# PSUM double buffering in a two-stage attention and expert kernel: wait for the reader of the own bank, not for the newest reader

## The reference

```python
xn = layernorm(x)
# recurrent stage: 8 heads of 128
q, k, v = xn @ Wq.T, xn @ Wk.T, xn @ Wv.T
o = chunked_linear_attention(q, k, v)          # causal, running state
o = rmsnorm(o / max(|sum(q * cumsum(k))|, 1))
s = o @ Wo.T
# gate stage
h1 = rmsnorm(xn) * g1
q = h1 @ fWq; c = h1 @ fWdkv                   # 1024 and 512 wide
k = c @ fWuk; v = c @ fWuv                     # 16 heads of 64
h2 = xn + softmax(causal(q @ k.T / 8)) @ v @ fWo
h3 = rmsnorm(h2) * g2
comb = softmax over the 2 best of 8 of (h3 @ gate_w), else 0
h4 = h2 + sum_e comb[:, e] * (silu(h3 @ w1[e]) @ w2[e])    # hidden 2048
y = x + s * silu(h4)
```

## Time and profile before

| | us |
|---|---|
| median of two runs | 6832.09 |
| the two runs | 6691.96, 6972.22 |
| profiled execution | 6699.76 |
| its span, slowest core | 6698.2 |
| spans of the 8 cores | 6643.8 to 6698.2 |
| TensorE matmuls busy | 3353.7 (50% of the span) |
| TensorE weight loads busy | 1259.4 (19%) |
| ScalarE busy | 1153.4 (17%) |
| VectorE busy | 1110.9 (17%) |
| GpSimd busy | 43.7 (1%) |

### The profile page before, as it was taken

How to read it: one execution, slowest core, us unless ns; L and a number is a source line. 1 busy time by engine, 2 the same in 40 slices (tenths; PEclk the granted TensorE clock), 3 DMA queues, 4 the chain that set the end, 5 groups by cost and what they waited for, 6 DMA issues and landing times.

```text
span 6698.2 us, 41992 instructions; the slowest of 8 cores (6643.8 to 6698.2 us)
## 1 busy us (share of the span) xinstructions
PE 3353.7 (50%) x13297; PEld 1259.4 (19%) x13297; DVE 1110.9 (17%) x2130; ACT 1153.4 (17%) x1783; POOL 43.7 (1%) x65
## 2 busy tenths in 40 slices
PE   0443333465233333333333447777777777777770
PEld 0221111211000000000001212222222222222220
DVE  4003333002222222222222210000000000000002
ACT  3221010110222222222222111110111111111111
POOL 0000000000000000000000000000000000000000
PEclk9976666675555555555555779998999999999995
DMA  4110000200000000000001120202020202020104
GB/s 151 35 25 10 13 13 13 41 13 7 0 0 0 0 0 0 0 0 0 0 0 28 43 43 1 50 0 51 0 51 0 51 1 51 3 49 15 36 1 150
DMA packets 56024, 158.52 MB, mean 24 GB/s; under 512 B 4224, under 2 KB 5248, under 8 KB 55808
## 3 DMA queue, kind: packets, MB, share of 16 engines
q0 software_dynamic: 39248, 95.54, 7.8%
q1 hardware_dynamic: 16560, 60.30, 2.6%
HBM read 209.42 MB, written 33.55 MB: 36 GB/s over the span
## 4 chain that ended last, share of the span: by engine, by line
PE 50%; DVE 16%; ACT 15%; issue 10%; DMA 6%; DVEq 1%; ACTq 1%; SPq 0%; POOLq 0%; PEldq 0%
PE ps L145 48%; ACT p2pb L803 7%; ACT p3hid L1012 5%; DVE p2rlf L831 3%; DVE acc L1031 3%; DMA p4s<-s_sp 1%; PE pt L150 1%; DMA p0x<-x 1%; DVE p2pb L815 1%; DVE p2pb L813 1%; DVEq L73 1%; DVE p1o1f L528 1%; PE pw L145 1%; DVE p2tmp L759 1%; DVE p2omla L846 1%
## 5 line engine op out<-in xcount | busy, mean ns | idle before, releaser
L145 PE MATMUL ps<-h3T,p3w 128*128 128x512 bf16 x4096 | 982.8, 383 | 435.2 <-ACT p3hid L1012 432.8
L145 PE MATMUL ps<-p3w,p3hid 128*128 128x512 bf16 x4096 | 935.5, 382 | 278.3 <-DVE acc L1031 241.7
L1012 ACT ACTIVATE p3hid<-ps 128x512 bf16<-128x512 f32 x512 | 305.7, 597 | 2276.8 <-PE ps L145 2276.8
L145 PE MATMUL ps<-p2pb,p2vaug 128*65 128x512 bf16 x640 | 302.0, 627 | 749.5 <-DVEq L96 414.3
L1031 DVE SCALAR_TENSOR_TENSOR acc<-ps,p3comb,acc 128x512 f32<-128x512 f32 x256 | 192.1, 750 | 2431.8 <-PE ps L145 2427.9
L145 PEld LDWEIGHTS ps<-h3T,p3w 128*128 128x128 bf16 x4096 | 369.1, 98 | 1043.5 <-issue 694.4
L803 ACT ACTIVATE p2pb<-ps,p2nmub 128x512 bf16<-128x512 f32 x640 | 439.9, 687 | 663.5 <-PE ps L145 617.7
L145 PEld LDWEIGHTS ps<-p3w,p3hid 128*128 128x128 bf16 x4096 | 384.5, 98 | 829.2 <-issue 428.3
L145 PE MATMUL ps<-p2qT,p2kT 64*128 64x512 bf16 x640 | 300.1, 622 | 138.8 <-DVEq L96 138.1
L145 PEld LDWEIGHTS ps<-p2pb,p2vaug 128*65 128x65 bf16 x640 | 87.7, 161 | 968.6 <-issue 968.6
L831 DVE RECIPROCAL p2rlf<-ps 1x512 f32<-1x512 f32 x64 | 214.7, 3355 | 153.9 <-PE ps L145 153.9
(11 more groups left out here) (154 smaller groups left out, 1828.6 us busy)
## 6 DMA issues: line engine op xcount, KB each, us to landing
p3w<-w POOLq DMA_DIRECT2D x16, 4096.0 KB, 25.5
p0x<-x SPq DMA_DIRECT2D x16, 512.0 KB, 4.2
xn_sp<-p0xn SPq DMA_DIRECT2D x16, 512.0 KB, 2.9
h_sp<-p0h1b POOLq DMA_DIRECT2D x16, 512.0 KB, 2.9
s_sp<-p1sout SPq DMA_DIRECT2D x16, 512.0 KB, 2.6
p2xnr<-xn_sp SPq DMA_DIRECT2D x16, 512.0 KB, 3.3
p4x<-x SPq DMA_DIRECT2D x16, 512.0 KB, 4.4
p4s<-s_sp SPq DMA_DIRECT2D x16, 512.0 KB, 5.4
```

The lines of the kernel that those rows point to most:

```text
L145: t.matmul(o, l, r, start=st, stop=sp), sig=sig)
L1012: e.activation(hv[:, m, :], pb[:, 0:512], AF.Silu), sig=True)
```

## The change

Every loop that alternates between two banks keeps, for each bank, the mark of the instruction that empties it, and the next group on that bank waits for that mark. The first group on each bank has no such wait. The same edit is made at six places: both projB, the v projection, the out-projection, and the hidden and the output groups of the experts. At the out-projection the signal of the first of the two additions is asked for too.

```diff
     def projB(dstv, wv, kk, n_mt):
+        bmark = [None, None]
         for m0 in range(n_mt):
             for sl in range(4):
-                pb = c.ps[sl % 2]
-                sch.wait("tensor", sch.mark("scalar"))
+                par = sl % 2
+                pb = c.ps[par]
+                if bmark[par] is not None:
+                    sch.wait("tensor", bmark[par])
                 for k in range(kk):
...
                          e.copy(d, p[:, 0:512]), sig=True)
+                bmark[par] = sch.mark("scalar")
...
+    vmark = [None, None]
     for i in range(NTI):
         for sl in range(2):
-            pb = c.ps[sl % 2]
-            sch.wait("tensor", sch.mark("vector"))
+            par = sl % 2
+            pb = c.ps[par]
+            if vmark[par] is not None:
+                sch.wait("tensor", vmark[par])
...
+            vmark[par] = sch.mark("vector")
...
+    h2mark = [None, None]
...
             for sl in range(2):
                 pb = c.ps[sl % 2]
-                sch.wait("tensor", sch.mark("vector"))
+                if h2mark[sl] is not None:
+                    sch.wait("tensor", h2mark[sl])
...
-                                      c.ps[sl][:, 0:512]), sig=(sl == 1))
+                                      c.ps[sl][:, 0:512]), sig=True)
+                h2mark[sl] = sch.mark("vector")
...
+    hmark = [None, None]
+    ymark = [None, None]
     for e_ in range(NEXP):
...
             for m in range(16):
-                pb = c.ps[m % 2]
-                sch.wait("tensor", sch.mark("scalar"))
+                par = m % 2
+                pb = c.ps[par]
+                if hmark[par] is not None:
+                    sch.wait("tensor", hmark[par])
...
                          e.activation(hv[:, m, :], pb[:, 0:512], AF.Silu), sig=True)
+                hmark[par] = sch.mark("scalar")
...
                 for dsl in range(2):
-                    pb = c.ps[2 + (tt * 2 + dsl) % 2]
-                    sch.wait("tensor", sch.mark("vector"))
+                    ypar = (tt * 2 + dsl) % 2
+                    pb = c.ps[2 + ypar]
+                    if ymark[ypar] is not None:
+                        sch.wait("tensor", ymark[ypar])
...
                                  OP.mult, OP.add), sig=True)
+                    ymark[ypar] = sch.mark("vector")
```

## The result

The changed kernel takes 5648 us where the kernel before takes 6681 (means; the medians are 5647 and 6674): 0.845 of it, 95% interval 0.844 to 0.847. In some executions of either kernel the cores of a die, or a pair of them, spend part of the expert stage at a lower clock (6972 was one of these); the comparison leaves them out. The forecast was 6080 with a range of 5900 to 6150. The direction was right and the size was not: about 1030 us came off, I had expected about 600. The time is that of the rival to which I gave 0.08, "the clock holds", 5680.

The account below looks back on a forecast made before the run. No engine is full; the engines take turns, with TensorE waiting for bank readers. From 6698 us, 424 (782 - 380 + 22) in the expert stage and 197 in the projections come off: 6077, said as 6080, range 5900 to 6150.

Parts of the forecast that it names:

- the clock holds: Rival: the clock stays at 1.00 in the expert stage despite denser matmuls; 5680 us, chance 0.08.
- The hand-overs: Expert stage: removing 480 waits for the Silu gains 506 us and 224 for the accumulation 276, together 782.
- What the density does to the clock: Expert stage: denser matmuls bring the clock to 0.81 throughout; 380 us come back, less 22 that core 5 already pays.
- my second argument: For 0.81: two unprofiled runs differ by 280 us, about what 0.81 over three quarters of the expert stage would cost.
- Weight loads: Expert w1 and w2 prefetches: cost nothing, but their cover shrinks to 8 us, or 2 at full clock.
- Eight-matmul projections: First-stage q and k, second-stage q and c: gaps worth 113 us, less 21 for the clock, net 92.
- k and v: Four-matmul k and v projections: gains of 51 and 54 us if the clock climbs from 0.50, otherwise 32 and 37.
- Out-projection: Out-projection with the residual: no gain, since both banks' waits already name a mark that has been reached.
- It brings nothing, since banks disturb each other: Rival: matmuls into one bank slow while another is read, so the gap returns; 6690 us, chance 0.01.
- The cross-check: Expert stage built up from nothing, 8192 x 0.262 plus 42, 5 and 2: 2195 us, beside 2201 by subtraction.

Follow-up runs that it names:

- pipelined version: Changed kernel with split hand-over, own-bank attention waits, and each query block's normalisation emitted behind the next block's first step: 4706 us, 0.704 of the kernel before.

## Why the prediction was wrong, point by point

- **The hand-overs.** Right. 480 x 1.055 = 506 us forecast, 516 measured by itself; 224 x 1.23 = 276 forecast, 289 measured. The waits named in the earlier trace rows vanish one by one with their edit.
- **The clock, "What the density does to the clock".** This is the step that failed: 0.81 for the whole stage, a term of 380 us. In the profiled execution it never had to be paid: the stage lasts 1813 us and not 2201. With the term, less the 22 that core 5 had lost before, the stage's gain came out at 424 in place of 804. The row of 0.81 was real, and its price of 0.262 us a matmul too, but I read it as a load two thirds of the way to a limit. The runs show a thing that strikes some executions and passes others by, at both densities: the changed kernel at 98% busy lost nothing in 11 of 16 executions, twice the stage can keep it too, and zeros in the operands take the long stretches away where the density is the same. The trace spoke against me as well: core 0 sat at 1.00 at the same moment under the same load, and I gave that a twelfth of the chances. Core 0 is on the other die, but core 6, on core 5's own die, was at 1.00 too, as was core 7. The 280 us between two runs, my second argument, were the mark of a disturbed execution, and no measure of the load. Core 6, before the change, columns as in the earlier trace rows:

```profile
4580.00:4660.00 80.00, 58.36 (x255) 23.07 (x252) 6.01 (x8) 9.00 (x16) 0.00 (x0) 1.00 0.25 47
```

- **The Trainium skill's rule** (TensorE: Matmul & The Clock Gate, section Seeing it yourself), that three cores of a die with dense matmuls bring the whole die to 13/16 for as long as the load lasts. The runs disagree for this kernel as a rule for every execution: eight cores at 98% for 3590 us at 1.00; and where the clock falls, pairs of cores fall, not always the die. Two of 20 executions look as the rule has it. The same section says that the limit depends on the data and that all-zero operands don't trip it. The runs agree that it depends on the data; with zeros in one operand of each matmul stretches at 0.81 still came, but no execution of twelve lost more than 42 us.
- **Weight loads.** Right. In the changed kernel TensorE has no wait for p3w; the cover of 2 us at full clock was real, since taking off the 1.3 us at a block's end makes the first waits appear, and loading w1 twice costs 18 to 27 us a time.
- **Eight-matmul projections.** The gap right: 113 forecast, and from the evictions' first and last starts 31.6 + 33.6 + 33.4 + 18.9 = 117 measured. The half charge of 21 us for the clock was the same mistake again.
- **k and v.** Right in kind and nearly in size: 51 and 54 forecast, 54.3 and 56.9 measured. The clock does come up once the gaps are gone. With the eight-matmul projections they sum to 228 us, within the 227 to 252 that the projections bring alone.
- **Out-projection.** Right: 1.003, and its interval of 0.999 to 1.007 holds no change.
- **It brings nothing, since banks disturb each other.** No: the pitch is 0.2159 us while ScalarE or VectorE reads the other bank in nearly every group. The Trainium skill's report (TensorE: Matmul & The Clock Gate, section HAM oscillation) of a double buffer without gain is of one other kernel, and doesn't carry over here.
- **The cross-check.** Building the stage up from nothing gave 2195 against 2201 and looked like a confirmation. Both carried the same 0.262 and so could not test it. With 0.2159 the same sum is 8192 x 0.2159 + 42 + 7 = 1818; from 3679.74 to the end of the last accumulation at 5493.2 it is 1813.

## What to carry to other kernels

When a loop alternates between buffers, the wait ahead of a group must name the reader of its own buffer; a wait for the engine's newest mark makes two buffers work as one wherever that mark is the other buffer's reader, and its price can be read off before the change as gap times count, to 5% here. Price a state of the chip that a profile shows only now and then as a chance, not as a term of the sum: ask first whether a core under the same load at the same moment escapes it, on the same die above all. And once the gaps are gone, look at what they covered: here the weight loads had 2 us left.

## What the runs showed of the hardware that I had not expected

- The stretches at 0.81 differ between pairs of cores: mean clocks of 0.776 and 0.775 on cores 4 and 5, 0.783 and 0.784 on 6 and 7, 0.793 to 0.795 on 0 to 3 in one execution. They last from a few us, beside a load, to a whole doubled stage (766 us lost), and with zeros in one operand of each matmul they cost at most 42 us in twelve executions.
- After 24 us without a matmul the granted clock is 0.50, and eight us after the return it is 1.00; the blocks behind seven such pauses took 1.5 to 2.7 us more.
- In the attention TensorE is busy for 80% of the time in the pipelined version and stays at 0.50, while the k projection is at 0.92 on average over its 35 us. The attention's matmuls use 64 or 65 of 128 rows or columns; whether that is the reason wasn't tested.
